# Attention output turned in 32x32 blocks by VectorE, LayerNorm's last step on ScalarE, layer 1's ternary weights made early and kept as int8

## What is computed

```python
x = layernorm(x + attn0(x))      # 16 heads of 16, causal, no biases
x = layernorm(x + ffn0(x))       # silu(x Wg^T * gs) * (x Wu^T * us), then Wd^T * ds; 704 wide
x = layernorm(x + attn1(x))      # the same attention with biases
x = layernorm(x + ffn1(x))       # silu(x q(Wup)^T) * (x q(Wgate)^T), then q(Wdown)^T; 1024 wide

def layernorm(x): return (x - mean) / sqrt(var + 1e-5)
def q(w):                        # ternary, one scale for the whole matrix
    scale = mean(abs(w)) + 1e-8
    return clip(round(w / scale), -1, 1) * scale
```

## Time and profile before

| | us |
|---|---|
| median of 3 runs | 269.2 |
| profiled execution | 269.13 |
| its span, first to last instruction | 267.4 |
| outside its span | 1.73 |
| PE busy / DVE busy / ACT busy / POOL busy | 248.4 / 211.8 / 153.9 / 159.2 |

### The profile page before, as it was taken

The page is one execution under the profiler, slowest core; times in us unless marked ns, Lnnn a source line. Parts: engine busy times, 40 slices in busy tenths (PEclk is TensorE's granted clock), DMA queues, the critical chain, the costliest instruction groups (busy, mean ns, idle before and its releaser), DMA issues.

```text
span 267.4 us, 6860 instructions
## 1 busy us (share of the span) xinstructions
PE 248.4 (93%) x2502; PEld 222.9 (83%) x2502; DVE 211.8 (79%) x688; ACT 153.9 (58%) x284; POOL 159.2 (60%) x176
## 2 busy tenths in 40 slices
PE   8789779999999999999999979989999999999990
PEld 7689757777898999889999878576689788999980
DVE  2466999858678955859899988999999884988574
ACT  3576228799643166955545268887585764434430
POOL 8767247789613145822562799839924894626361
PEclk9999999999999999999999999999999999999997
DMA  5998762762000004426400035670130000010102
GB/s 163 287 260 207 206 182 89 199 174 84 2 0 4 1 4 115 123 72 167 157 2 0 6 84 157 214 182 4 25 137 4 2 1 2 0 42 0 42 1 78
DMA packets 20146, 23.26 MB, mean 87 GB/s; under 512 B 2833, under 2 KB 17681, under 8 KB 19729
## 3 DMA queue, kind: packets, MB, share of 16 engines
q1 hardware_dynamic: 19968, 22.56, 29.9%
q10 hardware_dynamic: 144, 0.26, 0.3%
HBM read 9.05 MB, written 1.05 MB: 38 GB/s over the span
## 4 chain that ended last, share of the span: by engine, by line
PE 64%; DVE 13%; DMA 6%; issue 5%; POOL 4%; ACT 3%; SPq 3%; POOLq 0%; DVEq 0%; ACTq 0%
PE pair L524 10%; PE pair L525 9%; PE pair L526 9%; PE pair L700 6%; PE pair L701 5%; PE pair L631 4%; DVE block_max L947 4%; PE pair L614 4%; DMA raw<-a 2%; PE pair L592 2%; PE pair L641 2%; PE pair L724 2%; PE pair L725 2%; PE pair L634 2%; SPq L499 2%
## 5 line engine op out<-in xcount | busy, mean ns | idle before, releaser
L1131 POOL TENSOR_TENSOR hidden<-hf,hidden 128x512 fp32r<-128x512 f32 x28 | 36.2, 1294 | 41.0 <-ACT hidden L836 40.9
L794 ACT ACTIVATE probs<-pair 128x768 f32<-128x768 f32 x64 | 49.5, 813 | 13.9 <-PE pair L616 6.9
L1115 POOL TENSOR_SCALAR_AFFINE_SELECT probs<-probs 128x512 f32<-128x512 f32 x64 | 44.7, 712 | 16.6 <-ACT probs L794 16.0
L955 DVE CUSTOM_DVE_ANT_0 masked<-pair,mask 128x256 bf16<-128x256 f32 x80 | 33.4, 417 | 2.0 <-PE pair L593 1.8
L614 PE MATMUL pair<-q_stack,k_stack 98*128 98x256 bf16 x128 | 26.5, 274 | 4.5 <-ACT probs L794 2.2
L836 ACT ACTIVATE hidden<-hf 128x512 fp32r<-128x512 f32 x28 | 17.7, 630 | 16.4 <-DVE hf L1034 11.7
L1024 DVE SCALAR_TENSOR_TENSOR hf<-th,pair 128x512 f32<-128x512 f32 x28 | 19.1, 683 | 8.7 <-ACT th L828 4.9
L524 PE MATMUL pair<-xT_hi,gu_hi 128*128 128x256 f32 x88 | 25.5, 289 | 0.0
L525 PE MATMUL pair<-xT_lo,gu_hi 128*128 128x256 f32 x88 | 24.9, 283 | 0.0
L526 PE MATMUL pair<-xT_hi,gu_lo 128*128 128x256 f32 x88 | 24.9, 283 | 0.0
L616 PE MATMUL pair<-q_stack,k_stack 98*128 98x128 bf16 x128 | 23.7, 218 | 0.0
(11 more groups left out here) (156 smaller groups left out, 898.2 us busy)
## 6 DMA issues: line engine op xcount, KB each, us to landing
q_stack<-q_part SPq DMA_DIRECT2D x48, 128.0 KB, 2.7
k_stack<-k_part SPq DMA_DIRECT2D x48, 128.0 KB, 2.7
raw<-f SPq DMA_DIRECT2D x3, 1024.0 KB, 4.9
raw<-a SPq DMA_DIRECT2D x8, 256.0 KB, 3.7
raw<-f0gu SPq DMA_DIRECT2D x4, 352.0 KB, 3.5
x<-x_nat SPq DMA_DIRECT2D x4, 256.0 KB, 5.8
out<-x SPq DMA_DIRECT2D x4, 256.0 KB, 2.4
raw<-f0dn SPq DMA_DIRECT2D x3, 256.0 KB, 3.4
```

The lines of the kernel that those rows point to most:

```text
L794: nc.scalar.activation(probs[(n - 1) % 4][:, :, :], place(key)[:, :, 0:T + P], ACT.Exp, scale=SC).then_inc(exp_done, 1)
L955: nc.vector.tensor_tensor_reduce(out=masked[:, j, 0:T], in0=o[:, 0:T], in1=mask[:, 0:T], scale=1.0, scalar=NEG, op0=ALU.add, op1=ALU.max, ...
L1115: pool.affine_select(out=diag, in_=diag, compare_op=ALU.is_ge, fill=0.0, base=0, pattern=[[0, 2], [0, 2], [1, P]], channel_multiplier=-1). ...
L1131: pool.tensor_tensor(hidden[(n - 1) % NHID][1][:, :, :], hf[n % 2][:, :].rearrange("p (a t) -> p a t", a=2), hidden[(n - 1) % NHID][0][:, ...
```

## The change

1. **u and y^T turned by DVE.** UT and YT leave TensorE. A new VectorE instruction, `transpose`, turns a tile in 32x32 blocks. UT, now a DVE step for each PV tile, turns it straight from PSUM into u_t (128x256); ACT's copy L801 is gone. IV takes two reciprocals of 128x8, YM two products of 128x128 elements, both from u_t in SBUF, for each of two halves of a batch; YB turns y_t (128x512) into yT. The features come out in another order, for which the columns of the O weights and layer 1's bias are permuted on the host. ACT makes yT_hi from yT; the subtraction for yT_lo moves from DVE to POOL.
2. **LN's last step on ACT.** DVE negates the mean (one more 128x2 instruction), POOL multiplies it by the power (`offset`, one more 128x2 instruction), and ACT computes res * rstd + offset in two 128x256 instructions. DVE's next residual but one waits until they are done.
3. **Layer 1's ternary weights early.** raw is used in quarters after PREP0: 24 loads of 256 KB for the three matrices in place of three of 1 MB (each matrix is loaded twice, for AB, the absolute values, and for TERN), in a ring of two. Gate and up are staged as int8 in raw's second half, and ACT converts them (CV, eight 128x512 copies) into gu_hi and gu_lo once layer 0 is done with these.
4. **Masks.** MASKED_BY_PE goes from 3 to 4, and in those batches DVE reduces both heads of a step in one instruction.
5. **Order.** All five step tables and BANKS are written anew.

```diff
-MASKED_BY_PE = 3
+MASKED_BY_PE = 4
...
-TERN = 6
+PIECES = ([("PREP0", n) for n in range(PREP0)] + [("PREP1", n) for n in range(3)] + [("AB", n) for n in range(12)]
+          + [("TERN", n) for n in range(8)] + [("PREP1", 3)] + [("TERN", n) for n in range(8, 12)])
...
+        staged = raw[:, 1024:2048].bitcast(mybir.dt.int8)
...
@@ block.sync, RAW @@
+                    elif i < PREP0 or i >= PREP0 + 2:
+                        sp.wait_ge(*raw_used(PIECES[i - 2]))
...
@@ block.scalar @@
-                if step == "PV":
...
-                    nc.scalar.activation(u_sb[:, i, :], place(key)[:, 0:T], ACT.Copy).then_inc(u_done, 1)
...
+                if step == "LN":
+                    n = nth("LN", l, b)
+                    act.wait_ge(rstd_done, n)
+                    for tt in range(TT):
+                        last = nc.scalar.activation(x[:, TT * b + tt, :], res[n % 2][:, tt, :], ACT.Identity,
+                                                    scale=rstd[n % 2][:, tt:tt + 1], bias=offset[n % 2][:, tt:tt + 1])
+                    last.then_inc(ln_done, 1)
...
+                if step == "CV":
+                    n = CONVERTED[i]
+                    m, c = columns_of(n)
+                    act.wait_ge(tern_done, n + 1)
+                    act.wait_ge(gu_mm, nth("GU", 0, NB - 1, MT0 // 2 - 1))
+                    nc.scalar.activation((gu_hi, gu_lo)[m][:, c], staged[:, 512 * n:512 * (n + 1)], ACT.Copy).then_inc(converted, 1)
...
@@ block.vector @@
+                if n > 2:
+
+                    dve.wait_ge(ln_done, n - 2)
...
+                nc.vector.tensor_scalar(mv[k_][:, :, 0], mv[k_][:, :, 0], -1.0, None, ALU.mult)
...
+                        nc.vector.tensor_reduce(block_max[b % 2][:, 2 * i:2 * i + 2, 1:4],
+                                                both(key)[:, :, 0:3 * P].rearrange("p j (c t) -> p j c t", t=P),
+                                                mybir.AxisListType.X, ALU.max).then_inc(max_taken, 2)
...
+                    nc.vector.transpose(u_t[:, i, :], place(("PV", l, b, i))[:, 0:T]).then_inc(u_done, 1)
+                if step == "IV":
+                    dve.wait_ge(u_done, nth("PV", l, b, 2 * i + 1))
+                    for a in range(2):
+                        last = nc.vector.reciprocal(den_inv[:, 2 * i + a, :], by_token(2 * i + a)[:, :, HD])
+                    last.then_inc(inv_done, 1)
+                if step == "YM":
...
+                    for a in range(2):
+                        last = nc.vector.tensor_tensor(y_t[:, i, :].rearrange("p (c a d) -> p a c d", a=2, d=HD)[:, a, :, :],
+                                                       by_token(2 * i + a)[:, :, 0:HD],
+                                                       den_inv[:, 2 * i + a, :].unsqueeze(2).broadcast_to([P, T // 32, HD]), ALU.mult)
+                    last.then_inc(y_done, 1)
+                if step == "YB":
...
+                    nc.vector.transpose(yT[:, :, :].rearrange("p k t -> p (k t)"),
+                                        y_t[:, :, :].rearrange("p k t -> p (k t)")).then_inc(yT_raw_done, 1)
...
-                        ins = nc.vector.tensor_scalar(x[:, TT * b + tt, :], res[n % 2][:, tt, :], mv[n % 2][:, tt, 0:1],
-                                                      rstd[n % 2][:, tt:tt + 1], ALU.subtract, ALU.mult)
...
@@ block.gpsimd @@
+                    pool.wait_ge(power_done, n)
+                    pool.tensor_tensor(offset[n % 2][:, :], mv[n % 2][:, :, 0], rstd[n % 2][:, :], ALU.mult).then_inc(rstd_done, 1)
+                if step == "YT":
+                    pool.wait_ge(yT_hi_done, nth("YT", l, b))
+                    pool.tensor_tensor(yT_lo[:, :, :], yT[:, :, :], yT_hi[:, :, :].bitcast(fp32), ALU.subtract).then_inc(yT_done, 1)
```

350 lines of the change are left out of this document (165 added, 185 removed), and 15 rows, old and new, of the table BANKS.

## The result

The changed kernel is slower: 271.64 us (270.93 to 273.05) against 269.07 (268.56 to 269.27) beside it, a ratio of 1.0105 (95% interval 1.0059 to 1.0150). I had forecast 261.6. The profiled execution took 270.93 us and has a span of 269.2.

The account below looks back on a forecast made before the run. PE was taken as the bound except in layer 1's attention (DVE) and the tail; -3.3 - 1.0 + 2.0 - 3.5 - 2.6 + 0.9 = -7.5 on 267.4 gives 259.9, plus 1.73 outside the span 261.6 us; range 256.5 to 268.0.

Parts of the forecast that it names:

- -3.3: Layer 0: PE sets the pace, so 5.2 us less transposes and 1.9 us more mask matmuls save 3.3 us.
- +2.0: Layer 0, 34.4 to 123.8 us: DVE near full at 89% causes 2.0 us of new PE stalls (0 to 4).
- -3.5: Layer 1's attention: DVE, the bound, loses 2.7 us and POOL's comparisons leave the probs; 3.5 us saved (1 to 6).
- -2.6: Layer 1's feed-forward part, after 200.8 us: PE is the bound and loses two batches' transposes, saving 2.6 us.
- +0.9: Tail after the last power: a small POOL product, two ACT instructions for DVE's, and the negation add 0.9 us.
- -1.0: Layer 0's maxima around 34 to 45 us: reducing both heads in one instruction saves 1.0 us (0 to 1.7).
- The prices: DVE's division and transposes: 0.42 and 0.69 us a transpose, 0.29 a product, 0.2 a reciprocal; +1.8 us a batch.
- rival (c): DVE's transposes cost twice the rows' price, +2.4 us a batch: some 272 us, slower; 8% chance.
- rival (d): The weight ring of two quarters is too slow, ACT and PE run 8.5 us late: 270 us; 10% chance.
- (b): DVE sets everything: only its own -2.4 us and the tail's +0.9 count, 267.6 us; 12% chance.
- PE idle with all others idle too, a latency that I have hidden wrongly: Anywhere in the kernel: listed among signs that would show the forecast wrong; no size or chance of its own.

Follow-up runs that it names:

- the mended order: Changed kernel with SyncE issuing batch 1's q, middle and low stacks all before batch 2's q stack: 265.35 us, repeated 267.05, ratio 0.987 both times.
- experiment 7: Layer 0's mask products left out: of the mended order (128 products), 267.79 us, ratio 0.995; of the kernel before (96 products), 269.77 us, 1.002.
- experiment 5: Kernel before with only VectorE's transposes (change part 1): 288.66 us, ratio 1.072; the same without the softmax division: 275.04 us, 1.020.
- experiment 4: Softmax division (64 VectorE instructions) left out: of the changed kernel, 270.59 us, ratio 1.005; of the mended order, 265.56 us, 0.984.
- experiment 8: Mended order with layer 0's maxima taken head by head: 267.08 us, ratio 0.991; with the division in half as many instructions: 266.43 us, 0.989.

## Why the prediction was wrong, step by step

**The start, which isn't in the sum.** I opened it at 34.4 us, and took everything ahead of the first maxima as unchanged. But the change writes SyncE's order anew there, and I priced none of it; of the DMA I looked only at the engines' share, for the weight ring. This step, a term put at nothing without a reason, made 5.0 us of the changed kernel's span (6.0 against the mended order) and turned the sign: with the one move mended the kernel is 1.3% faster, where 2.8% had been forecast. Perfetto Trace Analysis (the Trainium skill, What "DMA-bound" means) names an issuing engine whose track is solid with DMA slices as a bound of its own, beside the DMA engines; the trace agrees, with an issue of 0.6 us every 0.65 us from 18.57 to 26.95.

**-3.3, TensorE's work in layer 0: wrong for its first part.** The step read "PE is busy 87.2 of 89.4 us: PE sets the pace". Busy 37.2 of 39.4 in the earlier trace rows is not working: by its starts TensorE stood 5.6 us there, and experiment 7 takes work away without a gain. From 73.8 to 123.8 us it stood only 0.9 of 50, and the reading holds: the stretch that answers to it is 10.7 us shorter with 11.2 us less work, part of it moved over the marks. The transposes themselves, taken from TensorE alone, gave nothing over all of layer 0 (experiment 5, 117.9 for 117.8 us). The +2.0 for a VectorE near full was right in sign; the stretches from 34.4 to 123.8 us stood 3.7 us longer (6.5 to 10.2).

**-3.5, layer 1's attention: wrong.** It rested on "DVE 94%, here DVE is the bound". The sum put VectorE at 69.5 us of work there and at 76.9 in layer 0's part; it was busy 77.2 and 71.4, so the new orders put more of it behind the mark than I had counted. In the changed kernel it is at 95% (77.20 of 81.20), the stretch is 81.2 us long for 77.0, and TensorE stands 9.6 us for 9.0. Taking 14 us of VectorE away moves little (experiment 4), taking GpSimd's 40 us away little more. Being full wasn't being last. All three middle stretches together: -5.8 forecast, -0.7 measured.

**-2.6, the feed-forward part of layer 1: right.** 59.7 to 56.7 us, -3.0. There TensorE really works 57.2 of 59.7 us, and less work is less time.

**+0.9, the tail: right in kind, about twice too large.** 6.9 to 7.4 us, +0.5; the small product takes 0.19 us, where 0.1 to 0.73 was expected. The rows answer to the earlier trace rows; timeline of the changed kernel:

```profile
264.07 0.16 DVE L908 TENSOR_SCALAR mv<-mv 128x2 f32<-128x2 f32 x1
264.31 0.69 POOL L1137 TENSOR_TENSOR rstd<-mv,minus_half 128x2 f32<-128x2 f32 x1 [2.34 <-DVE mv L908]
265.08 0.19 POOL L1139 TENSOR_TENSOR offset<-mv,rstd 128x2 f32<-128x2 f32 x1
265.31 1.09 ACT L815 ACTIVATE x<-res,offset,rstd 128x256 f32<-128x256 f32 x2 [2.21 <-POOL offset L1139]
```

From the power's start to x it is 2.1 us, where it was 1.5.

**-1.0, the merged maxima: not contradicted.** 1.1 by experiment 8, but with intervals that overlap.

**The prices.** Instructions of the changed kernel by line: shortest, median, longest in ns.

```profile
L998 DVE STREAM_TRANSPOSE u_t<-psum x32: 395/436/450, 52.1 to 232.4; 128x256 f32<-128x256 f32 x32
L1019 DVE STREAM_TRANSPOSE yT<-y_t x8: 662/700/712, 63.0 to 235.7; 128x512 f32<-128x512 f32 x8
L1010 DVE TENSOR_TENSOR y_t<-u_t,den_inv x32: 278/286/1399, 54.8 to 235.4; 128x128 f32<-128x128 f32 x32
L1002 DVE RECIPROCAL den_inv<-u_t x32: 139/158/206, 54.5 to 233.0; 128x8 f32<-128x8 f32 x32
L815 ACT ACTIVATE x<-res,offset,rstd x32: 584/593/605, 73.2 to 265.8; 128x256 f32<-128x256 f32 x32
L1139 POOL TENSOR_TENSOR offset<-mv,rstd x16: 194/195/197, 73.0 to 265.1; 128x2 f32<-128x2 f32 x16
```

Transposes at 0.44 and 0.70 us for 0.42 and 0.69, products 0.286 for 0.29, reciprocals 0.16 for 0.2, DVE busy 213.5 in 207 to 215: these held, and rival (c) fell. ScalarE's step was 0.59 for 0.47. What I had only in the range came: the mean of a product is 0.458, since some stretch to 1.4 us. All 13 over 0.3 us in the changed kernel stand beside GpSimd at work, ten beside the masking of exponentials, the two longest (1.27 and 1.40) beside hidden's split. Two timelines of the mended kernel show one beside yT_lo:

```profile
59.15 1.48 DVE L1010 TENSOR_TENSOR y_t<-u_t,den_inv 128x128 f32<-128x128 f32 x2
```

```profile
58.58 1.27 POOL L1142 TENSOR_TENSOR yT_lo<-yT,yT_hi 128x512 fp32r<-128x512 f32 x1
```

GPSIMD Engine Reference (the Trainium skill, Specifications) has GpSimd and VectorE instructions with two SBUF inputs share an interface; that agrees, and it now costs the products 32 x 0.17 = 5.5 us of VectorE (mean less median), as it cost LN before.

**The ring held, so rival (d) fell.** In these pieces POOL waits 2.2 us for loads into raw in all and ACT stands 0.1 us; groups of POOL and ACT:

```profile
L1176 POOL TENSOR_SCALAR below_of<-raw,of_matrix 128x512 bf16<-128x512 f32 x12 | 18.8, 1566 | 2.3 <-DMA raw<-f 2.2
...
L865 ACT ACTIVATE junk<-raw 128x512 bf16<-128x512 f32 x12 | 7.5, 623 | 0.1
```

**The rivals.** I had put 14% on slower, by (c) and (d) and "unforeseen waits in orders written anew". It was the last, which I had named but not looked for. Of the signs that I listed, the one that came true and led to the cause is "PE idle with all others idle too, a latency that I have hidden wrongly": from 28.0 to 32.6 us VectorE is busy 0.7 us, ScalarE 2.1 and GpSimd 2.0. The sign of (b), "PE idle with DVE full in both layers", can be read as well (VectorE at 92% and 95%), but experiment 4 speaks against (b) itself.

**What stays open.** Why the middle stretches stand 4.3 us more. VectorE's division, GpSimd's cut, SyncE's stacks of batch 3 and TensorE's mask products can each go without a gain worth naming. Five of these runs on the mended kernel show a fall of the clock between 39 and 46 us in their profiled execution, where its own two profiles have none: four for 3.4 us, which takes at most 1.7 us back, and the one without mask products for 6.8. A part of each gain may be lost there. I take it that with fixed orders on five queues another wait stands close behind each, but no run shows that.
